# Attention and BitNet feed-forward on eight cores: the input chain's small passes on ScalarE ahead of the third step's exponentials, the second residual half ahead of the masked maxima on VectorE

## The chip, the cores and the metric

The kernel runs on all 8 NeuronCores of one Trainium2 chip. Each core works on 2 of the 16 sequences, and the cores exchange nothing. The time is the device time of the slowest core in microseconds (us). Engines are called as in the profile: PE is TensorE, DVE is VectorE, ACT is ScalarE, POOL is GpSimd, and SP is SyncE, which issues DMA transfers.

## The reference

One layer on x of 16 x 2048 x 1024 in float32: layer norm, causal attention with a window of 128 keys and 16 heads of 64, residual; then layer norm, a feed-forward of two linear layers with ternary weights and 8-bit activations, residual.

```python
x = x + _L0_attn_ref(_layernorm(x), w_qkv, w_out)
x = x + _L0_ffn_ref(_layernorm(x), W1, b1, W2, b2)

def _layernorm(x, eps=1e-5):
    m = mean(x); v = var(x)
    return (x - m) / sqrt(v + eps)

# attention: scores = q k^T / 8, allowed = (j <= i) & (j > i - 128), softmax, times v, times w_out
# bitlinear: Wq = clip(round(W / mean|W|), -1, 1) * mean|W|
#            xq = clip(round(x * 127 / max|x|), -128, 127) * max|x| / 127
#            xq @ Wq^T + b;  between the two linears an exact gelu
```

## The kernel before, in words

A core has 32 tiles of 128 tokens (`nt` is 32), and the kernel has two stages. The first is attention: tile after tile, each in four steps, c = 0 to 3, so 128 steps that the code counts as j = 4t + c. A step handles four heads. The second stage is the feed-forward, which this change does not touch. During the attention stage the ternary weights of the feed-forward are made as well, in 128 small tasks that are spread over the steps: a weight tile of 128 x 1024 comes in by DMA into a staging buffer `stg`, and is either summed in absolute value (tasks a1, a2, on DVE or ACT) or quantized (tasks q1, q2: POOL scales it into `tern`, then DVE clips it and writes `W1q` or `W2q` in two passes, L704 and L706). The last 32 tasks, q2, come one in each step and have only two staging buffers.

No scheduler orders the work. Each helper appends its instruction to a queue of its engine (`QUEUE`, L175), with the semaphore values that it waits for, and the engines execute their queues strictly in that order. So the order of the calls in the loop at L969 is the order on each engine, and an instruction that waits holds up all that stands behind it on its engine. For SP and POOL that includes the DMA issues.

One step j of tile t issues, in this order of calls: the scores of the next step (`s_pe`, PE, names sc<-kT,qT); the masked maxima of the next step (`ttr`, DVE, L477, four custom instructions msc<-sc); the eviction left over from the last step (`prev_ev`); the exponentials of the next step (`ex`, ACT, probs<-msc, two before and two after the first filler); a first filler of matmuls and its eviction; the product with V of the step before (`av_pe`); the transposes of this step's probabilities (`t_pe`, PE into tA or tB) and their copy (`pt_ev`, PT); and a second filler of matmuls (`f2`), whose eviction `e2` becomes the `prev_ev` of the next step. The fillers are Q and K of the next tile at c = 0 and 1 (`qk_pe`, f<-xlnT,wqkv_sb), the output projection of the tile before at c = 2 (`o_pe`, f<-wout_sb,attnT), and V of the next tile at c = 3 (`v_pe`, f<-wqkv_sb,xlnT). There are two filler banks in PSUM, f0 and f1; the first filler writes f0, the second f1, and each waits until the bank's last content has been read (`ffree`).

The eviction of the output projection is `resid` (L589, recorded by L240, xr<-f,xr): DVE adds half a tile to the input x that lies in `xr` and sums it. Its first half runs within step c = 2; its second half is the `prev_ev` of step c = 3, where it stands behind the four masked maxima. The second filler of c = 3, the second half of V, waits for it, because it writes f1.

The input chain prepares tile t + 2 while tile t is in work. At the end of step c = 1 `ln1_stats` takes mean and variance on DVE (L335, L337, into `lnc`). In step c = 2 `ln1_rstd` makes the reciprocal deviation in two small ACT passes (Ln, Exp), behind the first two exponentials of that step; `ln1_nmr` makes minus mean times deviation on DVE (L349), behind the first residual half and the normalization `norm`; `xln_` applies both on POOL (xln<-xr,lnc); and `x_tr` transposes the result with a DMA from SP (L199, xlnT<-xln). The first Q matmuls of the next tile's step c = 0 wait for its landing. The transposed attention output (`at_tr`, attnT<-attn) takes the same way from step c = 0 to c = 2.

`task_pool` (L676) is POOL's part of a quantizing task for the next step; it stands at the head of the step, before `loads()`. `loads()` (L963) issues each weight load whose staging buffer's last reader has already been put in a queue: it is called in the middle of steps c = 0 and 2, and for the last 32 tasks at the head of steps 1 and 3 too.

Of the kernel before, what the change touches and what calls it, by code (L numbers as in the profile page):

```python
# [12 lines left out]
AF = mybir.ActivationFunctionType  # L13
# [29 lines left out]
def _build(nt):  # L43
# [99 lines left out]
    with ExitStack() as ctx:  # L143
# [68 lines left out]
        def act(out, in_, func, waits=(), bias=None, scale=None, accum=None):  # L212
            kw = {}
            if bias is not None:
                kw["bias"] = bias
            if scale is not None:
                kw["scale"] = scale
            if accum is not None:
                kw["accum_out"] = accum
            return op("act", lambda e: e.activation(out=out, in_=in_, func=func,  # L220
                                                    **kw), waits)
# [38 lines left out]
        def tok(*key):  # L260
            return tk.get(key if len(key) > 1 else key[0])
# [78 lines left out]
        def ln1_rstd(t):  # L340
            c = lnc[t % 2]
            b = act(c[:, 14:15], c[:, 13:14], AF.Ln,
                    [tok("mv", t), tok("konst")], bias=c_eps)
            tk["ln", t] = act(c[:, 15:16], c[:, 14:15], AF.Exp, [b],
                              scale=-0.5)

        def ln1_nmr(t):
            c = lnc[t % 2]
            tk["nmr", t] = op("dve", lambda e: e.scalar_tensor_tensor(  # L349
                out=c[:, 16:17], in0=c[:, 12:13], scalar=-1.0,  # L350
                in1=c[:, 15:16], op0=ALU.mult, op1=ALU.mult), [tok("ln", t)])

        def xln_(t):
            c = lnc[t % 2]
            tk["xln", t] = ts("pool", xln, xr[t % 5], c[:, 15:16], c[:, 16:17],
                              ALU.mult, ALU.add,
                              [tok("nmr", t), tok("ln", t), tok("x", t),
                               tok("xlnT", t - 1)])


# [512 lines left out]

        ln1_stats(0)
        ln1_rstd(0)
        ln1_nmr(0)
        xln_(0)
        x_pe(0)
        for i in range(4):
            piece_cast(i)  # L880
        ln1_stats(1)
        ln1_rstd(1)
        ln1_nmr(1)
        xln_(1)
        for i in range(4, 8):
            piece_cast(i)
# [82 lines left out]
        for j in range(nstep):  # L969
            t, c = j // 4, j % 4  # L970
            f1, e1 = fill(t, c, 0)
            f2, e2 = fill(t, c, 1)
            nxt = j + 1 < nstep
            mine = at_step[j]
            late = t == nt - 1

            if j == 5:
                tk["ones"] = memset("pool", ones, 1.0,
                                    [tok("w", 3, "a"), tok("w", 3, "v")])
            for n in at_step[j + 1] if nxt else ():  # L980
                if tasks[n][0][0] == "q":
                    task_pool(n)
            if j == 5 or (c in (1, 3) and to_load and to_load[0] >= 96):
                loads()
            if nxt:
                s_pe(j + 1)
                ttr(j + 1)
            if prev_ev is not None:
                prev_ev()
            if c == 3 and t >= 1:  # L990
                ln2_sum(t - 1)
                spill(t - 1)
            if nxt:
                ex(j + 1, 0)
                ex(j + 1, 1)
            if c == 0 and t >= 2:
                ln2_sq(t - 2)
            if c == (2 if t else 1) and t + 2 < nt:
                ln1_rstd(t + 2)
            if j == 2:  # L1000
                x_pe(2)
            if f1 is not None:
                f1()
                if c != 2 and not late:
                    e1()
            for n in mine:
                if tasks[n][0][0] == "a":
                    task_run(n)
            if c == 1:
                for n in mine:  # L1010
                    if tasks[n][0][0] == "q":
                        task_run(n)
            if nxt:
                ex(j + 1, 2)
                ex(j + 1, 3)
            if j >= 1:
                av_pe(j - 1)
            if c == 0 and t >= 1:
                norm(t - 1, 1)
                at_tr(t - 1)  # L1020
                if 2 <= t and t + 3 < nt:
                    load_x(t + 3)
                if j > 5:
                    loads()
            if c == 2 and f1 is not None:
                e1()
            if c == 2:
                norm(t, 0)
                if 1 <= t and t + 2 < nt:
                    ln1_nmr(t + 2)  # L1030
                    xln_(t + 2)
                    x_tr(t + 2)
                if j > 5:
                    loads()
            if j == 1:
                ln1_nmr(2)
                xln_(2)
            t_pe(j)
            pt_ev(j, on_act=((c == 2 and any(tasks[n][0][0] == "q"
                                             for n in mine))  # L1040
                             or (late and c < 2)))
            if late and c != 2:
                e1()
            if f2 is not None:
                f2()
            prev_ev = e2
            if c != 1:
                for n in mine:
                    if tasks[n][0][0] == "q":
                        task_run(n)  # L1050
            if c == (1 if t else 0) and t + 2 < nt:
                ln1_stats(t + 2)
            if j in sum_step:
                scale_sum(sum_step[j])
            if j - 1 in sum_step:
                scale_pe(sum_step[j - 1])
            if 1 <= j <= 4:
                for i in range(22 + 2 * j, 24 + 2 * j):
                    piece_cast(i)

            if t == nt - 3 and c == 3:
                load_x1(0)
                load_bias(0)
            if t == nt - 2:
                if c == 0:
                    ln2_rstd(0, nt - 4)
                    front_pool(0, [tok("task", n) for n in
                                   range(ntask - 2, ntask)])
                if c == 1:
                    load_x1(1)  # L1070
                    front_max(0)
                if c == 2:
                    front_q(0)
                    front_pool(1)
                if c == 3:
                    xt(0)
                    for i in range(1, 5):
                        load_bias(i)
            if late:
                if c == 1:  # L1080
                    load_x1(2)
                if c == 2:
                    for u in range(4):
                        gelu(0, u)
                    front_pool(2)
                if c == 3:
                    front_max(1)
                    front_q(1)
                    xt(1)
# [150 lines left out]
```

How the kernel before makes its waits and increments, by code:

```python
            def body(eng):  # L1175
                seen = {}
                for waits, fn, s, amt in QUEUE[q]:
                    for ws, val in waits:
                        if val > 0 and seen.get(ws.name, 0) < val:
                            eng.wait_ge(ws.h, val)
                            seen[ws.name] = val
                    if fn is None:
                        continue
                    ins = fn(eng)
                    if s is not None:
                        ins.then_inc(s.h, amt)
```

## Time and profile before

| | us |
|---|---|
| median of 3 runs | 1572.41 |
| lowest and highest | 1570.57, 1573.75 |
| the profiled execution's own time | 1578.92 |
| its span, slowest core (core 0) | 1577.3 |
| spans of the 8 cores | 1554.7 to 1577.3 |
| PE busy on core 0 | 1498.3 |
| DVE, ACT, POOL busy on core 0 | 1070.7, 794.3, 257.8 |

The span runs from a core's first to its last instruction; the execution's own time is 1.6 us more. Matmuls are pipelined and their ends are modelled, so that a short wait of PE can be hidden in its busy time; from one start to the next it can still be read. "Idle before, <- releaser" names what came last of the things that an instruction waited for. All eight cores run the same program, and differ by up to 22.6 us.

### The profile page before, as it was taken

How to read it: one execution, taken by the hardware profiler on the slowest of the kernel's cores; microseconds unless marked ns; L12 is line 12 of the kernel's file. 1: busy time of each engine (PE TensorE's matmuls, PEld its weight loads, DVE VectorE, ACT ScalarE, POOL GpSimd, SP SyncE). 2: the span in 40 equal slices, each digit the busy share in tenths (PEclk: the TensorE clock that was granted, in tenths of full speed). 3: DMA queues.
4: the chain of work that ended last, by engine and by line, in shares of the span. 5: the costliest groups of instructions: out<-in, count | busy, mean ns of one | idle time of the engine just before them, and what ended most of it. 6: DMA issues, size and time to landing. Idle time of an engine off the chain costs nothing.

```text
span 1577.3 us, 34004 instructions; the slowest of 8 cores (1554.7 to 1577.3 us)
## 1 busy us (share of the span) xinstructions
PE 1498.3 (95%) x11748; PEld 837.2 (53%) x11748; DVE 1070.7 (68%) x2693; ACT 794.3 (50%) x1832; POOL 257.8 (16%) x207
## 2 busy tenths in 40 slices
PE   3799889999999999989999999999999999999998
PEld 3566566666666666634444444444444444444443
DVE  2477769888888899777666666666666666666653
ACT  3577767777777777754433342333334233333421
POOL 0200003222223333103010101101010110101000
PEclk9899999999999999999999999999999999999999
DMA  9778977777776766434433434243444424334332
GB/s 293 223 178 228 195 209 229 215 215 200 210 200 165 193 190 195 104 102 105 100 82 80 101 71 109 61 91 90 81 100 71 111 61 97 85 80 101 68 80 54
DMA packets 275113, 213.74 MB, mean 136 GB/s; under 512 B 237184, under 2 KB 237312, under 8 KB 274944
## 3 DMA queue, kind: packets, MB, share of 16 engines
q1 hardware_dynamic: 270336, 194.79, 50.4%
q0 software_dynamic: 4608, 16.78, 2.7%
q8 instruction: 96, 1.57, 0.4%
q14 instruction: 73, 0.60, 0.1%
HBM read 120.29 MB, written 33.55 MB: 98 GB/s over the span
## 4 chain that ended last, share of the span: by engine, by line
PE 81%; DVE 7%; DMA 5%; issue 4%; SPq 2%; ACT 1%; POOL 1%; DVEq 0%; ACTq 0%; POOLq 0%
PE f L204 34%; PE av L204 30%; PE sc L204 15%; DVE msc L477 3%; DMA xlnT<-xln 2%; SPq L190 2%; DMA attnT<-attn 2%; DMA wst<-wqkv 1%; PE tB L209 1%; PE tA L209 1%; DVE xr L240 1%; DVE lnc L335 1%; ACT probs L220 1%; DVE tern L227 1%; POOL xln L227 1%
## 5 line engine op out<-in xcount | busy, mean ns | idle before, releaser
L204 PE MATMUL av<-W2q,hqT 128*128 128x512 fp8e4 x2048 | 447.2, 379 | 1.7 <-DVE msc L237 1.7
L220 ACT ACTIVATE hbuf<-hb 128x512 f32<-128x512 f32 x256 | 160.3, 629 | 450.0 <-DVE hb L237 450.0
L204 PEld LDWEIGHTS av<-W2q,hqT 128*128 128x128 bf16 x2048 | 200.5, 98 | 243.4 <-issue 2.2
L220 ACT ACTIVATE probs<-msc,cells 128x256 bf16<-128x256 f32 (+1 forms) x512 | 250.8, 491 | 94.1 <-DVE cells L477 93.6
L204 PE MATMUL f<-xlnT,wqkv_sb 128*128 128x128 bf16 x4096 | 256.9, 222 | 22.6 <-DMA xlnT<-xln 10.5
L204 PEld LDWEIGHTS f<-xlnT,wqkv_sb 128*128 128x128 bf16 x4096 | 238.3, 99 | 37.6 <-issue 37.4
L204 PE MATMUL f<-W1q,xlnT 128*128 128x512 fp8e4 x1040 | 235.6, 379 | 0.0
L204 PE MATMUL sc<-W1q,xlnT 128*128 128x512 fp8e4 x1008 | 227.8, 379 | 0.0
L477 DVE CUSTOM_DVE_ANT_0 msc<-sc,masks 128x256 f32<-128x256 f32 (+1 forms) x512 | 182.1, 411 | 43.5 <-PE sc L204 42.5
L220 ACT ACTIVATE hq<-hbuf,konst,fhc 128x1024 f16<-128x1024 f32 x128 | 148.4, 1229 | 89.2 <-DVE fhc L225 85.7
L204 PEld LDWEIGHTS f<-W1q,xlnT 128*128 128x128 bf16 x1040 | 101.3, 98 | 122.2 <-issue 0.4
L204 PEld LDWEIGHTS sc<-W1q,xlnT 128*128 128x128 bf16 x1008 | 98.5, 98 | 118.8
L237 DVE SCALAR_TENSOR_TENSOR hb<-f,fqc,b1b 128x512 f32<-128x512 f32 x128 | 95.7, 749 | 87.2 <-PE f L204 87.1
L245 DVE TENSOR_REDUCE fhc<-hbuf 128x1 f32<-128x1024 f32 x128 | 151.9, 1209 | 0.0
L227 POOL TENSOR_SCALAR stg<-xr,nmean 128x1024 f32<-128x1024 f32 x32 | 35.8, 1118 | 684.8 <-DMA xr<-x1sp 659.7
L204 PE MATMUL f<-wqkv_sb,xlnT 128*128 128x512 bf16 x512 | 123.1, 384 | 12.9 <-DVE xr L240 7.5
L225 DVE TENSOR_SCALAR hq<-hq 128x1024 bf16<-128x1024 f16 x128 | 55.8, 437 | 107.2 <-ACT hq L220 107.2
L204 PE MATMUL f<-wout_sb,attnT 128*128 128x512 bf16 x496 | 118.9, 383 | 9.6 <-DMA attnT<-attn 5.8
L227 POOL TENSOR_SCALAR tern<-stg,wsc 128x1024 bf16<-128x1024 f32 x64 | 74.3, 1161 | 159.9 <-DMA stg<-w1t 49.4
L220 ACT ACTIVATION_READ_ACCUMULATOR probs<-msc,cells 128x1 f32 x512 | 96.3, 188 | 0.0
L227 POOL TENSOR_SCALAR xln<-xr,lnc 128x1024 bf16<-128x1024 f32 x32 | 45.6, 1426 | 309.9 <-DVE lnc L349 154.9
L204 PEld LDWEIGHTS f<-wqkv_sb,xlnT 128*128 128x128 bf16 x512 | 45.8, 98 | 69.6 <-issue 24.3
(86 smaller groups left out, 1393.5 us busy)
## 6 DMA issues: line engine op xcount, KB each, us to landing
stg<-w1t SPq DMA_DIRECT2D x64, 512.0 KB, 8.5
stg<-w2t SPq DMA_DIRECT2D x64, 512.0 KB, 5.5
xr<-xc SPq DMA_DIRECT2D x32, 512.0 KB, 5.1
x1sp<-xr POOLq DMA_DIRECT2D x32, 512.0 KB, 6.5
xr<-x1sp SPq DMA_DIRECT2D x32, 512.0 KB, 4.6
y<-msc SPq DMA_DIRECT2D x31, 512.0 KB, 3.3
wst<-wqkv SPq DMA_DIRECT2D x24, 512.0 KB, 18.2
wst<-wout SPq DMA_DIRECT2D x8, 512.0 KB, 19.9
```

What stands on the lines that cost most here:

```text
L190: lambda e: e.dma_start(out=out, in_=in_), s, 16))
L204: return op("pe", lambda e: e.matmul(out=out, lhsT=lhsT, rhs=rhs, start=start, stop=stop), waits, sig)
L209: return op("pe", lambda e: e.transpose(out=out, in_=in_, identity=ident), waits, sig)
L220: return op("act", lambda e: e.activation(out=out, in_=in_, func=func, **kw), waits)
L225: return op(q, lambda e: e.tensor_scalar(out=out, in0=in0, scalar1=s1, scalar2=None, op0=op0), waits)
L227: return op(q, lambda e: e.tensor_scalar(out=out, in0=in0, scalar1=s1, scalar2=s2, op0=op0, op1=op1), waits)
L237: return op("dve", lambda e: e.scalar_tensor_tensor(out=out, in0=in0, scalar=s, in1=in1, op0=op0, op1=op1), waits)
L240: return op("dve", lambda e: e.scalar_tensor_tensor(out=out, in0=in0, scalar=s, in1=in1, op0=op0, op1=op1, accum_out=accum), waits)
L245: return op("dve", lambda e: e.tensor_reduce(out=out, in_=in_, axis=AX.X, op=o, apply_absolute_value=absv), waits)
L335: i=x[:, h * 512:(h + 1) * 512]: e.bn_stats(out=o, in_=i),
L477: e.tensor_tensor_reduce(out=u, in0=i, in1=m, scale=-0.125, scalar=BIG, op0=ALU.add, op1=ALU.min, accum_out=a), w)
```

## The change: order of three chains and one operation moved

The small pass L349 on DVE becomes a third small pass on ACT, an Identity with the deviation as its scale, which gives mean times deviation; POOL now subtracts it. The three ACT passes, POOL's normalization and the transposing DMA are issued at the head of step c = 2, behind the masked maxima in the code and ahead of the step's exponentials on ACT. The second half of the residual is issued ahead of the masked maxima in step c = 3. POOL's part of a quantizing task is issued behind all these, where it stood at the head of the step.

```diff
@@ -341,20 +341,15 @@
             c = lnc[t % 2]
             b = act(c[:, 14:15], c[:, 13:14], AF.Ln,
                     [tok("mv", t), tok("konst")], bias=c_eps)
-            tk["ln", t] = act(c[:, 15:16], c[:, 14:15], AF.Exp, [b],
-                              scale=-0.5)
-
-        def ln1_nmr(t):
-            c = lnc[t % 2]
-            tk["nmr", t] = op("dve", lambda e: e.scalar_tensor_tensor(
-                out=c[:, 16:17], in0=c[:, 12:13], scalar=-1.0,
-                in1=c[:, 15:16], op0=ALU.mult, op1=ALU.mult), [tok("ln", t)])
+            b = act(c[:, 15:16], c[:, 14:15], AF.Exp, [b], scale=-0.5)
+            tk["ln", t] = act(c[:, 16:17], c[:, 12:13], AF.Identity, [b],
+                              scale=c[:, 15:16])
 
         def xln_(t):
             c = lnc[t % 2]
             tk["xln", t] = ts("pool", xln, xr[t % 5], c[:, 15:16], c[:, 16:17],
-                              ALU.mult, ALU.add,
-                              [tok("nmr", t), tok("ln", t), tok("x", t),
+                              ALU.mult, ALU.subtract,
+                              [tok("ln", t), tok("x", t),
                                tok("xlnT", t - 1)])
 
 
@@ -873,14 +868,12 @@
 
         ln1_stats(0)
         ln1_rstd(0)
-        ln1_nmr(0)
         xln_(0)
         x_pe(0)
         for i in range(4):
             piece_cast(i)
         ln1_stats(1)
         ln1_rstd(1)
-        ln1_nmr(1)
         xln_(1)
         for i in range(4, 8):
             piece_cast(i)
@@ -977,26 +970,35 @@
             if j == 5:
                 tk["ones"] = memset("pool", ones, 1.0,
                                     [tok("w", 3, "a"), tok("w", 3, "v")])
-            for n in at_step[j + 1] if nxt else ():
-                if tasks[n][0][0] == "q":
-                    task_pool(n)
             if j == 5 or (c in (1, 3) and to_load and to_load[0] >= 96):
                 loads()
             if nxt:
                 s_pe(j + 1)
+            if c == 3 and prev_ev is not None:
+                prev_ev()
+                prev_ev = None
+            if nxt:
                 ttr(j + 1)
             if prev_ev is not None:
                 prev_ev()
             if c == 3 and t >= 1:
                 ln2_sum(t - 1)
                 spill(t - 1)
+
+            if c == 2 and 1 <= t and t + 2 < nt:
+                ln1_rstd(t + 2)
+                xln_(t + 2)
+                x_tr(t + 2)
+            for n in at_step[j + 1] if nxt else ():
+                if tasks[n][0][0] == "q":
+                    task_pool(n)
             if nxt:
                 ex(j + 1, 0)
                 ex(j + 1, 1)
             if c == 0 and t >= 2:
                 ln2_sq(t - 2)
-            if c == (2 if t else 1) and t + 2 < nt:
-                ln1_rstd(t + 2)
+            if t == 0 and c == 1:
+                ln1_rstd(2)
             if j == 2:
                 x_pe(2)
             if f1 is not None:
@@ -1026,14 +1028,9 @@
                 e1()
             if c == 2:
                 norm(t, 0)
-                if 1 <= t and t + 2 < nt:
-                    ln1_nmr(t + 2)
-                    xln_(t + 2)
-                    x_tr(t + 2)
                 if j > 5:
                     loads()
             if j == 1:
-                ln1_nmr(2)
                 xln_(2)
             t_pe(j)
             pt_ev(j, on_act=((c == 2 and any(tasks[n][0][0] == "q"
```

On ACT, in step c = 2 of a tile late in the attention stage (`lnc` is the input chain, probs<-msc the exponentials, kT the eviction of K). Before:

```order
L220 ACTIVATE kT_90<-f1 128x512
L220 ACTIVATE probs1_97,cells0_51<-msc1_95,cells0_51 128x256 x2
L220 ACTIVATE lnc0_53<-lnc0_53,konst_45 128x1
L220 ACTIVATE lnc0_53<-lnc0_53 128x1
L220 ACTIVATE probs1_97,cells0_51<-msc1_95,cells0_51 128x256 x2
L220 ACTIVATE PT0_98<-tB 128x1024
```

and with the change:

```order
L220 ACTIVATE kT_90<-f1 128x512
L220 ACTIVATE lnc0_53<-lnc0_53,konst_45 128x1
L220 ACTIVATE lnc0_53<-lnc0_53 128x1 x2
L220 ACTIVATE probs1_97,cells0_51<-msc1_95,cells0_51 128x256 x4
L220 ACTIVATE PT0_98<-tB 128x1024
```

The small passes are three and stand ahead of all four exponentials.

On DVE, at the change from step c = 2 to c = 3 of the same tile (ISA msc<-sc are the masked maxima, xr2,rsum<-f0 and f1 the two residual halves). Before:

```order
L240 SCALAR_TENSOR_TENSOR xr2_82,rsum_50<-f0,xr2_82 128x512
L250 RECIPROCAL cells0_51<-cells0_51 128x8
L232 TENSOR_TENSOR attn_100<-av,cells0_51 128x512
L349 SCALAR_TENSOR_TENSOR lnc0_53<-lnc0_53 128x1
L227 TENSOR_SCALAR tern1_109<-tern1_109 128x1024
L706 TENSOR_SCALAR W2q_61<-tern1_109 128x1024
L477 ISA msc0_94,cells1_52<-sc0,masks_44 128x256
...
L240 SCALAR_TENSOR_TENSOR xr2_82,rsum_50<-f1,xr2_82 128x512
```

and with the change:

```order
L240 SCALAR_TENSOR_TENSOR xr2_82,rsum_50<-f0,xr2_82 128x512
L250 RECIPROCAL cells0_51<-cells0_51 128x8
L232 TENSOR_TENSOR attn_100<-av,cells0_51 128x512
L227 TENSOR_SCALAR tern1_109<-tern1_109 128x1024
L701 TENSOR_SCALAR W2q_61<-tern1_109 128x1024
L240 SCALAR_TENSOR_TENSOR xr2_82,rsum_50<-f1,xr2_82 128x512
L472 ISA msc0_94,cells1_52<-sc0,masks_44 128x256
```

L349 is gone, and the residual half that reads f1 stands ahead of the maxima.

On SP, in the part with the last 32 tasks (stg<-w2t are weight loads). Before:

```order
L199 DMA_TRANSPOSE xlnT1_87<-xln_85 128x8x128
L190 DMA stg0_102<-w2t 128x1024
L190 DMA stg1_103<-w2t 128x1024
L199 DMA_TRANSPOSE attnT_101<-attn_100 128x8x128
L190 DMA xr4_84<-xc 128x1024
L190 DMA stg0_102<-w2t 128x1024
L190 DMA stg1_103<-w2t 128x1024
```

and with the change:

```order
L199 DMA_TRANSPOSE xlnT1_87<-xln_85 128x8x128
L190 DMA stg1_103<-w2t 128x1024
L190 DMA stg0_102<-w2t 128x1024
L199 DMA_TRANSPOSE attnT_101<-attn_100 128x8x128
L190 DMA xr4_84<-xc 128x1024
L190 DMA stg1_103<-w2t 128x1024
L190 DMA stg0_102<-w2t 128x1024
```

There are still two loads behind each transposing DMA, but the row of loads has moved by one: the weight tile that was loaded second behind one transposing DMA now comes first behind the next one.

## Rows read from the trace of the kernel before

**Rows 1.** The page's head: the span.

```profile
span 1577.3 us, 34004 instructions; the slowest of 8 cores (1554.7 to 1577.3 us)
```

**Rows 2.** The page's chain that ended last, by engine.

```profile
PE 81%; DVE 7%; DMA 5%; issue 4%; SPq 2%; ACT 1%; POOL 1%; DVEq 0%; ACTq 0%; POOLq 0%
```

**Rows 3.** Waits of PE, core 0, 100 to 668 us: total us, times, longest us.

```profile
PE f L204 <- DMA xlnT<-xln: 8.2, 5, 5.7
PE f L204 <- DVE xr L240: 7.5, 15, 1.2
...
PE f L204 <- ACT probs L220: 3.8, 2, 2.1
```

**Rows 4.** The same of core 1, 100 to 662 us.

```profile
PE f L204 <- DVE xr L240: 8.9, 17, 1.4
...
PE f L204 <- DMA xlnT<-xln: 0.3, 1, 0.3
```

**Rows 5.** Timeline, core 0, late in attention: start us, duration us, [idle before <-releaser].

```profile
581.59 0.21 DVE L337 BATCH_NORM_AGGREGATE lnc<-lnc 128x2 f32<-128x12 f32 x1
...
583.33 0.28 ACT L220 ACTIVATE lnc<-lnc,konst 128x1 f32<-128x1 f32 x1
583.70 0.20 ACT L220 ACTIVATE lnc<-lnc 128x1 f32<-128x1 f32 x1
583.81 0.49 ACT L220 ACTIVATE probs<-msc,cells 128x256 bf16<-128x256 f32 x1
...
584.84 0.15 DVE L349 SCALAR_TENSOR_TENSOR lnc<-lnc 128x1 f32<-128x1 f32 x1
584.91 0.42 DVE L227 TENSOR_SCALAR tern<-tern 128x1024 bf16<-128x1024 bf16 x1
...
585.35 1.70 POOL L227 TENSOR_SCALAR xln<-xr,lnc 128x1024 bf16<-128x1024 f32 x1 [3.09 <-DVE tern L227]
...
586.07 0.41 DVE L477 CUSTOM_DVE_ANT_0 msc<-sc,masks 128x256 f32<-128x256 f32 x1
...
586.92 0.61 PE L209 MATMUL tA<-identb,probs 128*128 128x128 bf16 x8
...
587.18 1.23 SPq L199 DMA_TRANSPOSE xlnT<-xln  x1
...
587.44 0.68 DVE L240 SCALAR_TENSOR_TENSOR xr<-f,xr 128x512 f32<-128x512 f32 x1
...
588.27 1.89 PE L204 MATMUL f<-wqkv_sb,xlnT 128*128 128x512 bf16 x8 [0.74 <-DVE xr L240]
...
588.55 0.50 ACT L220 ACTIVATE probs<-msc,cells 128x256 bf16<-128x256 f32 x1
```

**Rows 6.** The same timeline, the next tile's first step.

```profile
590.46 0.72 PE L204 MATMUL f<-xlnT,wqkv_sb 128*128 128x128 bf16 x10
...
592.47 0.61 PE L209 MATMUL tB<-identb,probs 128*128 128x128 bf16 x8
592.92 1.95 PE L204 MATMUL f<-xlnT,wqkv_sb 128*128 128x128 bf16 x32
```

**Rows 7.** The landings of xlnT, 100 to 660 us, and the late one, on PE.

```profile
DMA to landing us min/median/max: 3.0/3.1/9.2
...
200.38 1.86 PE L204 MATMUL f<-xlnT,wqkv_sb 128*128 128x128 bf16 x16 [5.72 <-DMA xlnT<-xln]
```

**Rows 8.** Weight loads and tasks late in attention, timelines of SP, POOL and DVE.

```profile
576.38 2.64 SPq L190 DMA_DIRECT2D stg<-w2t  x2
...
581.14 1.12 POOL L227 TENSOR_SCALAR tern<-stg,wsc 128x1024 bf16<-128x1024 f32 x1 [2.53 <-DMA stg<-w2t]
...
593.95 1.15 DVE L227 TENSOR_SCALAR tern<-tern 128x1024 bf16<-128x1024 bf16 x1
```

**Rows 9.** The page's median time to landing of the first matrix's weight loads.

```profile
stg<-w1t SPq DMA_DIRECT2D x64, 512.0 KB, 8.5
```

**Rows 10.** Groups of ACT: the table loads.

```profile
L220 ACT ACT_TABLE_LOAD x4 | 5.1, 1283 | 12.4 <-DVE lnc L337 6.7 <-DVE hb L237 5.6
```

## The prediction, as put on record

> **What bounds the kernel now.** I read the page first, then PE's waits in the attention stage, then the timeline of one tile, then the queues around it. The execution that was profiled has a span of 1577.3 us on its slowest core, and the other cores come in up to 22.6 us sooner [rows 1]. The chain that ended last is 81% PE [rows 2], so an edit on DVE, ACT or POOL pays only where PE waits for it. Between 100 and 668 us PE waits 8.2 us in 5 places for the transposed input xlnT, and 7.5 us in 15 places for the residual on DVE [rows 3]. On core 1 the second wait is there as well, 8.9 us in 17 places, but the first is only 0.3 us [rows 4]. The feed-forward stage is not touched, so these two waits are what there is to win.
>
> The timeline shows how both come about [rows 5, 6]. The variance is ready at 581.80 (581.59 + 0.21). The two small ACT passes start at 583.33 and 583.70, DVE's small pass L349 at 584.84, POOL's normalization at 585.35, the transposing DMA at 587.18. The typical landing is 3.1 us after the issue [rows 7], so at about 590.3, and the Q matmuls that need it start at 590.46. This chain of 8.5 us ends just as PE wants it, with nothing to spare; where the landing is late, PE stands (5.72 us at 200.38, the longest landing being 9.2 us [rows 7]). And in step c = 3 the masked maxima start at 586.07, the residual half behind them at 587.44, and the second half of V starts only at 588.27. Without the wait it would have started 0.45 us after the transposes before it, which is how far 592.92 is from 592.47 [rows 6]: at 586.92 + 0.45 = 587.37. So 0.90 us are lost where the row says 0.74; the modelled end of the transposes hides 0.16.
>
> **The change part by part.**
>
> Residual ahead of the maxima. DVE has the residual half's input already: the output projection ends before the scores for which the maxima wait, since PE does them in that order. The half would start at 586.07 instead of 587.44 and be done at about 586.8, ahead of 587.37. The wait goes: 7.5 us, and 15 times the hidden 0.16, 2.4 us, make 9.9 us. What is late next are the four maxima, by 0.6 to 0.7 us (0.68, the length of the half). They feed exponentials of which the last starts at 588.55 and ends with its accumulator read at about 589.1; the transposes that need it start at 592.47, or 591.6 once the 0.90 us are gone. That leaves over 1.5 us of cover. If ACT had another 1.2 us of work there the cover would shrink to nothing, and 0.7 us a tile, 20 us over 29 tiles, would be at stake; I take nothing of it. The sum and mean behind it and the spill's issue on POOL do not come later.
>
> The input chain. The third ACT pass is not in this trace in this form. From below it costs no more than the small Exp, 0.20 us; from above the first, with its bias, 0.28 us; I take 0.20, as it has no bias, just a scale. Passes that depend on each other start 0.37 us apart (583.33 to 583.70), so all three are done about 0.37 + 0.3 + 0.2 = 0.9 us after the variance, at 582.7, and POOL could start at about 582.9 instead of 585.35. That is 2.4 us sooner. POOL's subtract instead of add is one operation for another of the same size: I take no difference, and bound it by the spread that the rows show for the same tile work, 1.11 to 1.70 us. The DMA lands 2.4 us or more before PE asks for it, and all waits for a typical landing go. Of the one of 5.72 us about 2.7 us may stay, since the landing itself was 6.1 us over the typical. So of 8.2 us I count 5.5. On ACT the third pass adds 0.2 us per tile, 28 tiles. It delays the first two exponentials of step c = 2 by 0.3 to 0.5 us, because they now wait for the small passes, and not the last two, since the two old passes stood between them before (583.81 follows 583.70). The transposes that need all four start at 586.92, over 2 us later: hidden. The DVE pass, 0.15 us, goes too, 28 times, from an engine that has slack in most tiles: nothing counted.
>
> The quantizing tasks. POOL's part is now behind the normalization in step c = 2 and behind the spill in step c = 3, and at steps 1 and 3 it is recorded only after `loads()`. So in the last 32 tasks each odd step's load moves on to the next even step. A load that went out as the second behind the transposing xlnT DMA now goes out first behind the transposing attnT DMA. The pair issued at 576.38 brings such tiles [rows 8]: its first landed when POOL could start at 581.14, 4.8 us later. In the new order this first one belongs to the task that DVE clips at 584.91 [rows 5]; 581.1 and 1.1 us on POOL make 582.2, so 2.7 us are left, and the normalization behind it on POOL, ready at 582.9, is not held up. The next pair would go out at about 585.5, behind the earlier transposing DMA, land at 590.3 and be through POOL at 591.4; DVE wants it at 593.95 [rows 8], 2.5 us later. Nothing queued behind these waits on SP is delayed, as the pair's second load waits for a task that is done by then. I take zero.
>
> DVE's clip of 593.95 took 1.15 us and the one of 584.91 took 0.42: in the first case POOL was at its own task from 593.71 to 594.82 [rows 5, 8]. The Trainium skill states the reason (SBUF — State Buffer, section "Who interferes with whom"): the two engines share a port pair, which one instruction holds for its whole length. The trace agrees, and by this rule moved POOL tasks may slow other DVE passes or spare them. The cost is 0.73 us a meeting. A meeting more in each of the 9 tiles with a tight DVE would be 7 us at the very most, one less as much gained; which of the two the new order gives cannot be read before, and I take zero in the middle.
>
> Sum against the profiled execution: 9.9 + 5.5 = 15.4 us on core 0. On core 1 it is 8.9 + 17 x 0.16 + 0.3 = 11.9 us. The slowest core need not be the same one, and a PE that waits less reaches other limits sooner (3.8 us of waits put down to ACT [rows 3] show that there are some). I take 13 us: 1578.9 becomes 1565.9. The profiled execution was 6.5 us over the median of the runs, 1572.4; from that median it is 1559.4 us.
>
> **The rivals.**
>
> DVE takes over as the limit. For it speaks that in the tile shown the maxima start at 586.07, about a microsecond after their scores, so DVE is behind, and a shorter period of PE finds no shorter one of DVE. Against it: DVE loses 0.15 us of work and its meetings with POOL may get fewer. Then half of the residual's 9.9 us comes back as other waits and half of the input chain's: a gain of 5 to 7 us, about 1566.
>
> The waits are hidden anyway, or all come back. The wait for xlnT is there on some cores only [rows 3, 4], and if the later maxima eat what the earlier residual gives, there is a change of no more than 3 us: 1572.
>
> Slower, by weight loads that come late. The last 32 weight tiles have lost most of a step of lead. From the issue to the landing the rows show 4.8 us here, but the other weight matrix has a median of 8.5 us [rows 9]. At 8.5 us the first load is through POOL at 576.4 + 8.5 + 1.1 = 586.0, 1.1 us after DVE wants it, and the second at 595.1, 1.2 us late. Both are waits in the middle of DVE's queue, in front of the residual half and the maxima. That is 2.3 us in each of 9 tiles, 21 us, against which only the gains of the other tiles stand, some 9 us: 1584. It decides from a landing time of 7.4 us; the one load of this kind in the rows stays 2.6 us under it.
>
> Slower, by table loads. ACT loads a function table 4 times in all, 1.28 us each [rows 10]. If the Identity next to Exp and Ln made it load two in every tile, ACT would lose 2.6 us in step c = 2, against a cover of 2 us, and 0.6 us or more in 28 tiles would be lost, 17 us, to be set against the 13: 1576. The Trainium skill says (ScalarE: Activation LUTs, section "Table sets: the hidden batching unit") that cheap functions, identity among them, are in every set. By that rule nothing is loaded; the trace has Identity only in the feed-forward, beside Gelu, and so does not show it.
>
> **How the numbers follow.** The forecast, both waits gone, gets 68%: 1553 to 1565, with 1559.4 as its value. DVE as the limit gets 16%: 1563 to 1568. No change gets 8%: 1569 to 1576. Late loads get 5% and table loads 3%. Two runs of this kernel can be told apart from about 0.2%, 3.1 us. So faster has 0.68 + 0.16 and 0.01 of the near-zero case, 0.85; the same 0.08; slower 0.07. The range goes from 1552.5, which is all of core 0's waits with the hidden parts and 2 us of allowance for the start of the program, to 1569, which takes in the second case and the edge of the third.
>
> **What the changed profile would show.** PE's waits for xr (L240) fall from 7.5 us to under 1.5, and the second half of V starts 0.45 us after the transposes. The transposing DMA of xlnT is issued at least 2 us earlier against the end of the variance (5.4 us before, under 3.5 after), and PE's waits for it are under 3 us. PE's busy time stays within a few us and the attention stage ends 12 to 16 us sooner, the feed-forward takes as long as before. ACT still loads 4 tables. I am wrong if DVE is seen waiting for POOL's tern, if the transposes of step c = 0 wait for ACT, or if the gaps before V have only moved to the scores or to the output projection.

## The result

| | before | changed |
|---|---|---|
| median | 1571.49 us of 4 runs | 1599.38 us of 4 runs |
| profiled execution's span, slowest core | 1577.3 | 1596.7 |
| PE busy on that core | 1498.3 | 1498.9 |
| POOL busy on that core | 257.8 | 333.2 |

The change makes the kernel slower: the ratio is 1.0179, with a 95% interval from 1.0144 to 1.0214. I had forecast 1559.4 us in a range from 1552.5 to 1569. Medians, here and below, are of the executions in which neither half of the chip's cores ran at a lower clock than the other.

The page's head and its row on the engines of the changed kernel answer to [rows 1] and to the table above; the second row is busy us, share of the span, and number of instructions.

```profile
span 1596.7 us, 34118 instructions; the slowest of 8 cores (1576.9 to 1596.7 us)
PE 1498.9 (94%) x11748; PEld 843.0 (53%) x11748; DVE 1068.5 (67%) x2661; ACT 798.9 (50%) x1864; POOL 333.2 (21%) x207
```

PE and DVE work as long as before. POOL works 75 us more with the same 207 instructions. The chain that ended last, which was 81% PE and 1% POOL [rows 2], now goes through POOL's pass and the DMAs:

```profile
PE 77%; DMA 7%; DVE 4%; POOL 4%; issue 3%; ACT 2%; SPq 2%; DVEq 0%; ACTq 0%; POOLq 0%
```

The waits of PE on core 0 between 100 and 690 us (total us, times, longest us) answer to [rows 3]:

```profile
PE f L204 <- DMA xlnT<-xln: 19.2, 9, 4.9
PE f L204 <- ACT probs L220: 11.6, 8, 2.3
PE f L204 <- ACT junk L220: 3.1, 1, 3.1
PE f L204 <- ACT vh L220: 2.6, 2, 1.4
PE f L204 <- DMA attnT<-attn: 2.2, 2, 1.3
```

The wait for the residual (DVE xr, 7.5 us before) is gone from the list, as forecast. The wait for xlnT has grown from 8.2 to 19.2 us instead of going, and most of what is put down to ACT seems to belong to it too: the tile below shows one such case, and on this core the Q matmuls start 0.25 us after the landing of xlnT in 25 of 29 tiles. So one of the two waits was won and the other more than doubled.

The tile of step c = 2 and 3 on the changed kernel's timeline (start us, duration us) is the one of [rows 5]:

```profile
580.29 0.21 DVE L337 BATCH_NORM_AGGREGATE lnc<-lnc 128x2 f32<-128x12 f32 x1
...
580.98 0.59 ACT L220 ACTIVATE lnc<-lnc 128x1 f32<-128x1 f32 x2
...
581.87 3.78 POOL L227 TENSOR_SCALAR xln<-xr,lnc 128x1024 bf16<-128x1024 f32 x1 [0.86 <-ACT lnc L220]
...
584.67 0.68 DVE L240 SCALAR_TENSOR_TENSOR xr<-f,xr 128x512 f32<-128x512 f32 x1
...
584.82 0.61 PE L209 MATMUL tA<-identb,probs 128*128 128x128 bf16 x8
...
585.51 1.89 PE L204 MATMUL f<-wqkv_sb,xlnT 128*128 128x512 bf16 x8
...
585.78 1.23 SPq L199 DMA_TRANSPOSE xlnT<-xln  x1
...
586.69 0.58 POOL L190 DMA_DIRECT2D x1sp<-xr  x1
...
589.08 1.95 PE L204 MATMUL f<-xlnT,wqkv_sb 128*128 128x128 bf16 x32 [1.36 <-ACT vh L220]
```

POOL starts 1.37 us after the variance (580.50), near the forecast 1.1, instead of 3.55 us. But its pass takes 3.78 us, so the transposing DMA goes out 5.28 us after the variance, and before it was 5.38. The whole move of the chain is eaten by this one instruction. Meanwhile PE arrives sooner, because the residual half now stands ahead of the maxima: the second half of V starts 0.69 us after the transposes instead of 1.35 (0.45 was forecast). The Q matmuls behind it then wait 1.36 us for the landing. The row names ACT vh, but that pass had ended; 585.78 and the usual 3.05 us to landing make 588.83, and PE starts 0.25 us later. Two summary rows of POOL's pass (durations in ns, min/median/max), first of the kernel before, then of the changed one:

```profile
L227 POOL TENSOR_SCALAR xln<-xr,lnc x32: 1179/1300/1700, 9.2 to 643.3; 128x1024 bf16<-128x1024 f32 x32
```

```profile
L227 POOL TENSOR_SCALAR xln<-xr,lnc x32: 3770/3775/4263, 9.7 to 661.2; 128x1024 bf16<-128x1024 f32 x32
```

That is 2.5 us more in each of 32 tiles. The landing has become slower as well; min/median/max on core 0 between 100 and 680 us, against 3.0/3.1/9.2 in [rows 7]:

```profile
DMA to landing us min/median/max: 3.0/3.7/8.3
```

So there were two things to explain: the pass, and the landing.

### The profile page after: what moved, and what is told of

Its sections match the earlier page's. It is cut to its first block, busy times and chain, and to the rows that moved or that the text cites. A ratio compares the mean times of both kernels' runs of the same rounds, so it can differ in the third digit from the quotient of the medians.

```text
span 1596.7 us, 34118 instructions; the slowest of 8 cores (1576.9 to 1596.7 us)
## 1 busy us (share of the span) xinstructions
PE 1498.9 (94%) x11748; PEld 843.0 (53%) x11748; DVE 1068.5 (67%) x2661; ACT 798.9 (50%) x1864; POOL 333.2 (21%) x207
## 4 chain that ended last, share of the span: by engine, by line
PE 77%; DMA 7%; DVE 4%; POOL 4%; issue 3%; ACT 2%; SPq 2%; DVEq 0%; ACTq 0%; POOLq 0%
PE f L204 31%; PE av L204 29%; PE sc L204 15%; DMA xlnT<-xln 3%; POOL xln L227 3%; DMA stg<-w2t 2%; SPq L190 2%; DVE msc L472 1%; DMA wst<-wqkv 1%; PE tA L209 1%; PE tB L209 1%; ACT probs L220 1%; DMA attnT<-attn 1%; ACT lnc L220 1%; DVE PT L253 1%
## 5 line engine op out<-in xcount | busy, mean ns | idle before, releaser
L204 PE MATMUL f<-xlnT,wqkv_sb 128*128 128x128 bf16 x4096 | 261.7, 225 | 49.3 <-DMA xlnT<-xln 25.7
L204 PEld LDWEIGHTS f<-xlnT,wqkv_sb 128*128 128x128 bf16 x4096 | 244.1, 101 | 63.5 <-issue 63.2
L227 POOL TENSOR_SCALAR xln<-xr,lnc 128x1024 bf16<-128x1024 f32 x32 | 123.4, 3857 | 322.5 <-ACT lnc L220 299.6
L232 DVE TENSOR_TENSOR attn<-av,cells 128x512 bf16<-128x512 f32 x64 | 44.3, 692 | 63.2 <-PE av L204 53.9
```

The lines of the kernel that those rows point to most:

```text
L204: return op("pe", lambda e: e.matmul(out=out, lhsT=lhsT, rhs=rhs, start=start, stop=stop), waits, sig)
L227: return op(q, lambda e: e.tensor_scalar(out=out, in0=in0, scalar1=s1, scalar2=s2, op0=op0, op1=op1), waits)
L232: return op(q, lambda e: e.tensor_tensor(out=out, in0=in0, in1=in1, op=o), waits)
```

## The experiments

Kernels that were run together shared a chip and the runs of the kernel before, whose median was between 1568.5 and 1577.6 us from one such group to the next. So the ratios to it are compared here, and not the times. "Spill late" means that the write of x1 to memory, on POOL's queue, waits for the landing of xlnT. The kernel with four forms of POOL's pass ran once and has no row.

| kernel | ratio to before | 95% interval |
|---|---|---|
| the change | 1.0179 | 1.0144 to 1.0214 |
| with add | 0.9869 | 0.9848 to 0.9889 |
| before, with subtract | 1.0762 | 1.0739 to 1.0784 |
| before, residual first | 1.0257 | 1.0188 to 1.0326 |
| chain alone, with add | 0.9892 | 0.9864 to 0.9920 |
| whole change, add and right sign | 0.9853 | 0.9829 to 0.9877 |
| before, residual first, spill late | 0.9964 | 0.9935 to 0.9993 |
| the change, spill late | 1.0096 | 1.0065 to 1.0127 |
| whole change with add, spill late | 0.9849 | 0.9832 to 0.9866 |
| whole change with add, tasks at head | 0.9856 | 0.9816 to 0.9896 |
| whole change, add then mult | 0.9861 | 0.9823 to 0.9899 |

**The change with add.** One word differs.

```diff
-                              ALU.mult, ALU.subtract,
+                              ALU.mult, ALU.add,
```

> The changed kernel with add in place of subtract as POOL's second operation, nothing else; its normalized input has the wrong constant for that reason. Theory S (the subtract form of POOL's pass, 3.77 us against 1.2 to 1.7 us before, is what costs): the pass takes 1.2 to 1.7 us again, the transposing DMA goes out about 2.9 us after the variance instead of 5.3, and the time is 1556 to 1563 us. Rival Q (the new order of the queues costs: the transposing DMA meets the spill and the weight loads, and the weight tiles come late): the pass is short but the time stays at or over 1572 us. Rival P (POOL is slow since DVE holds the port at the new place): the pass stays near 3.8 us.

Measured: 1547.84 us against 1568.5 of the kernel before. POOL's pass and then all waits of PE in attention, 100 to 631 us, on core 0 (granted clock 0.992):

```profile
L227 POOL TENSOR_SCALAR xln<-xr,lnc x32: 1184/1189/1447, 9.5 to 604.9; 128x1024 bf16<-128x1024 f32 x32
```

```profile
PE f L204 <- ACT qT L220: 0.8, 3, 0.5
PE f L204 <- DVE xr L240: 0.7, 1, 0.7
PE f L204 <- issue: 0.3, 1, 0.3
```

The forecast waits are gone. Theory S holds, and P and Q fall: the place is the same, the queues are in the same order, only the operation differs, and the difference is 3.1% of the time. The gain of 21 us is more than the 13 that I had forecast for the whole change, and more than theory S gave.

**The kernel before with subtract.**

```diff
-                out=c[:, 16:17], in0=c[:, 12:13], scalar=-1.0,
+                out=c[:, 16:17], in0=c[:, 12:13], scalar=1.0,
...
-                              ALU.mult, ALU.add,
+                              ALU.mult, ALU.subtract,
```

> The kernel before with subtract instead of add in POOL's pass (and the sign of the small DVE pass turned round), nothing moved. Theory S: the pass takes 3.77 us, the transposing DMA goes out 2.1 to 2.5 us later in each tile and PE, which had no slack at its landing, waits about that long in 28 tiles: 50 to 65 us more, 1620 to 1636 us. Rival P (the place makes it slow, not the operation): the pass takes 1.2 to 1.7 us and the time is 1572 us.

Measured: 1687.26 us, 119 us over the kernel before, twice what I had expected. The pass takes 3.77 us or more here too, 3.88 in the median on the slowest core (core 2), where the kernel before has 1.29. The waits of that core's PE, 100 to 774 us:

```profile
PE f L204 <- DMA xlnT<-xln: 58.4, 16, 4.5
PE f L204 <- ACT probs L220: 27.7, 11, 2.6
```

That is 86 us in 27 places, 3.2 us in each. The longer pass accounts for 2.6 of them, and the landing for the other 0.7: it takes 3.75 us in the mean on core 2, where the kernel before has 3.08. In 80 of the 200 tiles of the eight cores the spill of x1 now goes out 0.2 us ahead of the transposing DMA, and these landings took 4.4 to 5.7 us; the next experiment comes back to this.

The rest of the 119 us is TensorE's clock. Windows of that core (us, busy us of the engines with instructions, then the granted clock, DMA share and GB/s), here and then in the kernel before:

```profile
100.00:600.00 500.00, 416.84 (x4984) 311.28 (x5025) 351.77 (x1161) 318.06 (x958) 141.20 (x83) 0.93 0.66 173
```

```profile
100.00:600.00 500.00, 474.78 (x6132) 344.00 (x6182) 434.29 (x1444) 379.39 (x1163) 123.18 (x114) 1.00 0.77 208
```

With a wait of over 3 us in each tile the granted clock is 0.93 of 2.4 GHz on the mean, so that it stood at 1.2 GHz for part of the time; without it, 1.00. All eight cores show this, 0.90 to 0.97 in every stretch of 100 us up to 600 us. What it costs can be read from PE's busy time on core 2 over the whole span: 1522.9 us against 1481.9 for the same 11685 matmuls, 41 us more. I did not take either of the two into account.

**The kernel before with the residual first.**

```diff
+            if c == 3 and prev_ev is not None:
+                prev_ev()
+                prev_ev = None
+            if nxt:
                 ttr(j + 1)
```

> The kernel before with the residual's second half ahead of the masked maxima in step c = 3, nothing else. By the prediction's sum the wait for it (7.5 us listed, 9.9 us with the hidden part) is won: 1562 us. By theory X (in the trace of before PE starts the Q matmuls exactly 0.25 us after the landing of xlnT in nearly every tile, so the landing has no slack) the wait only moves there: PE's waits for xlnT grow by about what those for xr lose, and the time is 1568 to 1573 us.

Measured: 1611.59 us, 43 us slower, a ratio of 1.0257. Neither my sum nor theory X had that; X had the direction of PE's waits right and the size wrong. One tile on core 1, with the DMA issues (SPq, and POOL for the spill x1sp):

```profile
231.66 1.22 SPq L199 DMA_TRANSPOSE xlnT<-xln  x1
231.88 0.58 POOL L190 DMA_DIRECT2D x1sp<-xr  x1 [0.35 <-DVE cells L477]
...
239.09 2.19 PE L204 MATMUL f<-xlnT,wqkv_sb 128*128 128x128 bf16 x19 [2.72 <-DMA xlnT<-xln]
```

The residual's second half ends at 231.26 + 0.08, so the spill of x1, which POOL issues when that half is done, now goes out 0.2 us behind the transposing DMA (0.9 us in the median of the tiles). In the kernel before it went out 1.5 us behind it, in the median on every core. PE starts at 239.09, 0.25 us behind a landing as elsewhere, so xlnT took 7.2 us to land. On core 1 the landings, 100 to 690 us, are

```profile
DMA to landing us min/median/max: 3.0/3.9/7.2
```

where the same core of the kernel before had 3.0/3.1/5.0. The median distance of 0.9 us says little here, for the tiles fall into two groups. Over all eight cores, 88 of 230 tiles have the spill between 0.2 us ahead of the transposing DMA and 0.7 us behind it, and every one of these landings took over 4.5 us, 5.1 in the median; 136 have it 0.9 us behind, and their median is 3.1 us. The kernel before has no tile of the first group.

The 2.6% are not all due to the landings. Cores 0 and 1 of this execution had 0.81 and 0.80 of the clock between 100 and 200 us, and the other six, with landings as late, 0.97 to 1.00; why those two had less is not known, and they are the slowest. The median of all cores, over the executions compared, is 1584.3 us, where the kernel before has 1559.8: 1.6% more.

**The same with the spill behind the landing**, made to separate the spill from the rest.

```diff
                                  [tok("R", t, 0), tok("R", t, 1),
+                                  tok("xlnT", t + 3)])
```

> The kernel before with the residual half ahead of the maxima (which alone came to about 1615 us), and the spill of x1 on POOL's queue made to wait for the landing of xlnT. Theory D (the earlier residual lets the spill go out 0.9 us behind the transposing DMA instead of 1.5 us, and its 512 KB make the landing late, mean 4.4 us instead of 3.3): landings are 3.1 us again with a mean under 3.5 us, and the time is 1562 to 1573 us. Rival C (the landing is late for other reasons, or the cost is only that PE reaches the wait earlier): landings stay over 4 us in half of the tiles and the time stays over 1585 us.

Measured: 1568.17 us, a ratio of 0.9964 against 1.0257 without this line (by the median of all cores 0.996 against 1.016). Theory D holds: the spill beside the transposing DMA is the cause. On core 1 the landings, 100 to 640 us, are back:

```profile
DMA to landing us min/median/max: 3.0/3.1/4.8
```

The residual's move alone is then worth 0.4%, with an interval from 0.1 to 0.7%, where my sum had 0.6%.

**The change with the spill behind the landing**, same edit.

> The changed kernel as it is, with subtract, and only the spill made to wait for the landing of xlnT. Theory D: landings 3.1 us, mean mv-to-landing 8.4 us instead of 9.5, about 1 us less wait in 28 tiles: 1565 to 1577 us, near or under the kernel before, so that the subtract alone is not the whole loss. Rival: the subtract is all and the spill nothing: 1595 to 1600 us.

Measured: 1588.51 us, a ratio of 1.0096 against 1.0179, above what I expected. So the early spill costs the changed kernel some 0.8%, about 13 us (64 of its 232 tiles have the spill within 0.4 us of the transposing DMA, and all their landings took over 4 us). The subtract itself is the larger part: from 1.0096 to the 0.9849 of the whole change with add and the same late spill are 2.5%, about 39 us. And the early spill is the subtract's doing as well. With the chain moved and add, the spill is at least 0.9 us behind the transposing DMA in every tile, with the residual first or not; with subtract it comes close to it even where nothing has been moved.

**The chain alone, with add.** Against the whole change with add (next), only the residual is back behind the maxima.

```diff
-            if c == 3 and prev_ev is not None:
-                prev_ev()
-                prev_ev = None
```

> The changed kernel with the residual back behind the maxima, and with add on POOL: ACT makes minus the mean in a fourth small pass between Ln and Exp and multiplies that. Theory S: POOL's pass takes 1.2 to 1.7 us, xlnT lands 2 us or more before it is wanted, PE waits for xr as before (7 to 9 us), and only the waits for xlnT go: 1563 to 1569 us. Rival Q: 1572 us or more, since the queues are in the new order here as well.

Measured: 1552.71 us, a ratio of 0.9892, some 10 us better than expected. Of PE's waits on the slowest core nearly only the residual's are left:

```profile
PE f L204 <- DVE xr L240: 6.4, 13, 0.8
PE f L204 <- ACT kT L220: 1.0, 2, 0.6
```

The chain is the larger gain, and the residual adds 0.4% to it, which is not clear of the noise, as the two intervals overlap.

**The whole change with add and the right sign.** A fourth small ACT pass makes minus the mean in the pause between Ln and Exp.

```diff
+            m = act(c[:, 16:17], c[:, 12:13], AF.Identity, [tok("mv", t)],
+                    scale=-1.0)
             b = act(c[:, 15:16], c[:, 14:15], AF.Exp, [b], scale=-0.5)
-            tk["ln", t] = act(c[:, 16:17], c[:, 12:13], AF.Identity, [b],
+            tk["ln", t] = act(c[:, 17:18], c[:, 16:17], AF.Identity, [m, b],
                               scale=c[:, 15:16])
...
-            tk["xln", t] = ts("pool", xln, xr[t % 5], c[:, 15:16], c[:, 16:17],
-                              ALU.mult, ALU.subtract,
+            tk["xln", t] = ts("pool", xln, xr[t % 5], c[:, 15:16], c[:, 17:18],
+                              ALU.mult, ALU.add,
```

> The whole change with add on POOL, and the right sign by a fourth small ACT pass (minus the mean, between Ln and Exp): both waits of PE gone. Theory S: POOL's pass 1.2 us, the fourth pass costs ACT 0.2 us a tile and no time; as the kernel with add alone, 1545 to 1551 us. If the fourth pass is on the path, 28 times 0.1 to 0.3 us more: 1550 to 1557 us.

Measured: 1548.96 us, a ratio of 0.9853. It beats both kernels: 1.5% under the one before. POOL's pass:

```profile
L227 POOL TENSOR_SCALAR xln<-xr,lnc x32: 1184/1189/1195, 9.6 to 612.1; 128x1024 bf16<-128x1024 f32 x32
```

**The same with the spill behind the landing.**

> The whole change with add and the right sign, and the spill behind the landing of xlnT. The transposing DMA goes out 3 us ahead of the spill there already and PE hardly waits for it, so both theories expect the time of the same kernel without this wait, within 3 us.

Measured: 1549.81 us, a ratio of 0.9849: no difference. With the quick pass the transposing DMA is 3 us ahead of the spill anyway. By the landings counted above, it hurts where the two go out within 0.7 us of each other.

**Four forms of POOL's pass**, in the kernel before, by tile.

```diff
+            if t % 4 == 0:
+                tk["xln", t] = op("pool", lambda e: e.tensor_scalar(
+                    out=xln, in0=x, scalar1=r, scalar2=m, op0=ALU.mult,
+                    op1=ALU.add), w)
...
+            elif t % 4 == 2:
+                tk["xln", t] = op("pool", lambda e: e.tensor_scalar(
+                    out=xln, in0=x, scalar1=c[:, 12:13], scalar2=r,
+                    op0=ALU.subtract, op1=ALU.mult), w)
```

> The kernel before, with POOL's pass written in four forms that turn with the tile: t mod 4 = 0: x times r plus m' (mult, add); 1: x times r minus m r (mult, subtract); 2: x minus m, times r (subtract, mult); 3: x plus minus m, times r (add, mult). All give the reference's values. Theory F (subtract as an operation of POOL is slow wherever it stands): forms 1 and 2 take 3.8 us, forms 0 and 3 take 1.2 us. Rival G (one combination, mult then add, is quick and any other slow): forms 1, 2 and 3 take 3.8 us. Rival H (only subtract as the second operation is slow): form 1 alone.

Measured, one run of 1630.83 us; durations in ns, min/median/max, in the order of the four forms:

```profile
L363 POOL TENSOR_SCALAR xln<-xr,lnc x8: 1184/1694/1717, 9.7 to 628.4; 128x1024 bf16<-128x1024 f32 x8
L367 POOL TENSOR_SCALAR xln<-xr,lnc x8: 3783/3892/4291, 19.1 to 648.0; 128x1024 bf16<-128x1024 f32 x8
L371 POOL TENSOR_SCALAR xln<-xr,lnc x8: 3782/4288/4294, 64.4 to 670.8; 128x1024 bf16<-128x1024 f32 x8
L375 POOL TENSOR_SCALAR xln<-xr,lnc x8: 1181/1188/1695, 87.9 to 692.4; 128x1024 bf16<-128x1024 f32 x8
```

Theory F: both forms with a subtract are slow, wherever it stands, and both without are quick, in either order.

**The tasks back at the head of the step**, on top of the whole change with add.

> The whole change with add and the right sign, but POOL's part of the quantizing tasks back at the head of the step, ahead of the normalization. If the moved tasks have a share in the gain, since the normalization does not stand behind a task that waits for its weights or its buffer: the pass starts 1.2 us or more later in steps with a task, PE waits up to 5 us more and the time is 1552 to 1556 us. If they have none: 1547 to 1551 us.

Measured: 1553.31 us, a ratio of 0.9856, against 0.9853 with them moved. The time lies in the range of the first theory, but the kernel before was slower in this group too (1577.6 us), and by the ratios the move of the tasks has no share that can be told; the interval, 0.4% to either side, leaves room for one of some 6 us.

**Add first, then multiply.** The last experiment takes the quick form that the four forms pointed to: minus the mean is made beside the chain, and no pass multiplies the two.

```diff
+            m = act(c[:, 16:17], c[:, 12:13], AF.Identity, [tok("mv", t)],
+                    scale=-1.0)
...
-            tk["xln", t] = ts("pool", xln, xr[t % 5], c[:, 15:16], c[:, 16:17],
-                              ALU.mult, ALU.subtract,
+            tk["xln", t] = ts("pool", xln, xr[t % 5], c[:, 16:17], c[:, 15:16],
+                              ALU.add, ALU.mult,
```

> The whole change with POOL's pass as (x plus minus the mean) times the deviation: minus the mean is an Identity pass on ACT between Ln and Exp, and no pass multiplies the two, so ACT has three small passes as in the changed kernel and the reference's values come out. Theory F (add is quick in either position): POOL's pass 1.2 us, the transposing DMA 2.4 us after the variance instead of 2.7, no wait left to win: 1545 to 1551 us, a ratio of 0.983 to 0.987 to the kernel before. If the order of operations mattered: 3.8 us and over 1590 us.

Measured: 1548.79 us, a ratio of 0.9861. It is as good as the fourth pass on ACT, with one pass less.

## Why the prediction was wrong

**The step that failed** is the one on POOL's pass: "POOL's subtract instead of add is one operation for another of the same size: I take no difference, and bound it by the spread that the rows show for the same tile work, 1.11 to 1.70 us." It takes 3.77 us. The bound was no bound: all the tile passes it came from have mult and add, and none shows a subtract on POOL. The right reading of those rows would have been that subtract is not shown, with a range that has no upper end from them, and a rival of its own, as the pass stands on a chain that ends exactly when PE wants it.

**The chain without slack** was read rightly, and its value too low. I counted the listed 8.2 us less 2.7. But where a landing sets the start of PE in four tiles of five, a gain upstream is worth more than the listed waits: in the kernel before, PE starts the Q matmuls 0.25 us after the landing in 23 to 25 of about 30 tiles on every core, though only 5 are listed as waits on core 0. The chain alone with add gained 1.08%, 17 us, where its part of the sum was 5.5. With add the landing has the lead that I forecast: in the whole change with add and the right sign PE starts 2.2 to 2.7 us after it in the median of each core (2.4 forecast).

**The residual.** The wait went as forecast: it is not among the changed kernel's waits, and the second half of V starts 0.69 us after the transposes. What I said of the rest was "The sum and mean behind it and the spill's issue on POOL do not come later." True, and it was the wrong question: the spill came sooner, next to the transposing DMA, and made it land later. Residual first alone costs 2.6% on the slowest core and 1.6% on the median one; with the spill held back it gains 0.4%. In the changed kernel the early spill was the smaller part, some 0.8%, and there it needed the slow pass: with the chain moved and add, the transposing DMA is away before the spill comes.

**ACT.** The small passes start at 580.59 and end at 581.57, 1.07 us after the variance (0.9 forecast), and their cost is hidden: the whole change with add is as quick with four of them (0.9853) as with three (0.9861). The rival of table loads falls: the changed kernel has four, as in [rows 10], though Identity now stands beside Ln and Exp. So the trace agrees with the Trainium skill (ScalarE: Activation LUTs, section "Table sets: the hidden batching unit") that identity is in every set.

```profile
L220 ACT ACT_TABLE_LOAD x4 | 5.1, 1283 | 12.9 <-DVE lnc L337 7.2 <-DVE hb L237 5.6
```

**The weight loads.** I had named DVE waiting for POOL's tile as a sign of being wrong, and on core 0 of the changed kernel it is there, as it was not before:

```profile
DVE tern L227 <- POOL tern L227: 12.1, 8, 2.3
```

But this does not bear out the rival of late loads. With add and the right sign, and the loads in the same order, core 0 has no such wait and no core more than 6.3 us of it: most of it goes with the pass of 3.78 us that stands ahead of POOL's task. Nor did moving the tasks back to the head change the time. The rival of DVE as the limit falls too: with add, PE has under 2 us of waits on core 0.

**The clock** was in none of my cases. In the kernel before with subtract PE waits 3.2 us in each tile, the granted clock is 0.93 on the mean of 500 us, and PE is busy 41 us longer for the same matmuls; this is a third of its loss. In the changed kernel it plays a small part: 0.96 to 1.00 in the stretches from 100 to 700 us, and PE is busy no longer than before.

The sizes for the changed kernel against the kernel before, from the ratios: the chain with add and the residual first, minus 1.5% (0.9849); the subtract with the spill held back, plus 2.5% (1.0096); the early spill on top, plus 0.8% (1.0179). These are the steps of one row of kernels, so that their sum of 1.8% is no test of them, and each rests on one experiment. As the changed kernel with add has no such early spill, the whole way from 0.9853 to 1.0179, 3.3%, hangs on that one word.

## What to carry to other kernels

A swap of one arithmetic operation for another on an engine is a change of its own: price it by a row of that operation on that engine, and if there is none, say so and give it a rival. When a producer is made faster, list what its end releases, DMA issues above all, and ask what they will now stand next to; sooner can be worse. And a wait that stands in every tile at a fixed distance behind one landing marks a chain with no slack: work on it is worth more, and harm to it costs more, than the listed waits say.

## What the hardware showed that I had not expected

- A pass of 128 x 1024 on POOL from float32 to bfloat16 with two operations took 1.18 to 1.72 us with mult and add, in either order, and 3.77 to 4.29 us as soon as one of the two was a subtract.
- A spill of 512 KB issued close to a transposing DMA of another queue makes that DMA land late. In the changed kernel and in the kernel before with subtract and with the residual first, 232 tiles have it from 0.2 us ahead to 0.7 us behind: all of these landings took over 4.1 us, up to 8.3. At 0.9 us behind, most are at the usual 3.1 us. The Trainium skill (DMA: Bandwidth & Descriptors, section "Issuing engines are not separate DMA queues") says that transfers of all queues run on the same 16 DMA engines and interleave; the traces agree that they disturb each other, but why a lead of 0.9 us is mostly enough was not tried. Landings over 4 us also occur without a spill nearby (41 of 248 in the whole change with add and the right sign); what makes those late is open.
- PE's waits "until issue" are 7.5 us on core 0 before and 0.3 us there in the changed kernel with add. But in the whole change with add and the right sign core 4 has 4.3 us of them, so an early xlnT does not do away with them. What they are stays open.
- PE, with a wait of over 3 us in each tile, ran the same 11685 matmuls 41 us longer, at a mean granted clock of 0.93 between 100 and 600 us instead of 1.00.
